# Layer-normed rows turned by one DMA per batch instead of by TensorE, and probabilities of two heads turned by one DMA

## The reference, cut to what matters

```python
h = jnp.maximum(_layernorm(x), 0.0)                  # no gain, no bias
q, k, v = split_heads(h @ Wq.T), split_heads(h @ Wk.T), split_heads(h @ Wv.T)
a = einsum('bhnd,bhmd->bhnm', q, k) * 512 ** -0.5 + (adj + adj)[:, None]
row_nonzero = any(a != 0, axis=-1)
p = softmax(where(row_nonzero, a, -inf)); p = where(isnan(p), 0, p)
o = einsum('bhnm,bhmd->bhnd', p, v)                  # heads put side by side
return x + o @ Wo.T
```

## Time and profile before

| | us |
|---|---|
| median of three runs (lowest, highest) | 1005.39 (1004.05, 1005.59) |
| the profiled execution's own time | 1005.16 |
| its span in the profile | 1003.4 |
| busy: PE, ACT, POOL, DVE | 959.6, 934.5, 862.3, 850.0 |
| transposing DMAs issued: heads, weights | 512, 4 |

### The profile page before, as it was taken

One profiled execution on the slowest core, in us unless ns is written; L12 is line 12 of the kernel. 1 busy time (PEld: TensorE's weight loads), 2 busy tenths in 40 slices (PEclk: granted clock), 3 DMA queues, 4 the chain that ended last, 5 costly groups with the idle time before them and its releaser, 6 DMA issues.

```text
span 1003.4 us, 33752 instructions
## 1 busy us (share of the span) xinstructions
PE 959.6 (96%) x11580; PEld 660.2 (66%) x11580; DVE 850.0 (85%) x3092; ACT 934.5 (93%) x3049; POOL 862.3 (86%) x936
## 2 busy tenths in 40 slices
PE   5879999999999999999999999999999999999965
PEld 4656776666677666777666677766666776667632
DVE  6778998888989888898988889988889898888863
ACT  5799999999999999999999999999999999999992
POOL 2278998989998898999888899989889988889894
PEclk9989999999999999999999999999999999999979
DMA  6289999999999999999999999999999999999995
GB/s 251 49 148 195 183 190 194 183 193 186 190 191 184 195 178 187 194 199 180 192 177 198 183 203 184 189 194 178 198 183 197 186 191 193 177 185 176 175 175 119
DMA packets 573818, 183.62 MB, mean 183 GB/s; under 512 B 547024, under 2 KB 555216, under 8 KB 573648
## 3 DMA queue, kind: packets, MB, share of 16 engines
q1 hardware_dynamic: 573648, 181.48, 100.9%
HBM read 29.36 MB, written 16.78 MB: 46 GB/s over the span
## 4 chain that ended last, share of the span: by engine, by line
PE 56%; DVE 28%; issue 8%; ACT 5%; POOL 1%; DMA 1%; DVEq 0%; POOLq 0%; ACTq 0%; SPq 0%
PE ps L1045 35%; DVE logits L752 15%; PE ps L1113 9%; PE ps L1063 7%; DVE stats L649 4%; ACT probs L547 3%; PE ps L942 3%; DVE q_lo L815 2%; DVE o_norm L782 2%; PE ps L1089 1%; DVE some L770 1%; ACT p L560 1%; PE ps L1019 1%; DMA w_nat<-in_L_gnn_Wq 1%; DVE row_min L752 1%
## 5 line engine op out<-in xcount | busy, mean ns | idle before, releaser
L430 POOL TENSOR_TENSOR p<-probs,p 128x512 f16<-128x512 f32 x512 | 586.4, 1161 | 89.9 <-ACT p L560 89.7
L547 ACT ACTIVATE probs<-logits,row_min 128x256 f32<-128x256 f32 x1024 | 513.6, 511 | 3.8 <-DVE row_min L752 3.8
L752 DVE CUSTOM_DVE_ANT_0 logits<-ps,adj_s,sigma 128x256 f32<-128x256 f32 x1024 | 438.0, 475 | 7.1 <-PE ps L1063 7.0
L560 ACT ACTIVATE p<-probs 128x512 f16<-128x512 f32 x512 | 323.5, 632 | 0.0
L1045 PE MATMUL ps<-ht_hi,w_hi 128*128 128x256 f16 x1024 | 280.2, 274 | 7.7 <-DVE q_lo L815 2.6
L1045 PE MATMUL ps<-ht_lo,w_hi 128*128 128x256 f16 x1024 | 279.4, 273 | 0.0
L1045 PE MATMUL ps<-ht_hi,w_lo 128*128 128x256 f16 x1024 | 279.4, 273 | 0.0
L547 ACT ACTIVATION_READ_ACCUMULATOR probs<-logits,row_min 128x1 f32 x1024 | 209.8, 205 | 0.0
L1045 PE MATMUL ps<-wo,o_hi 128*128 128x512 f16 x496 | 149.2, 383 | 3.8 <-POOL o_lo L456 3.8
L1045 PEld LDWEIGHTS ps<-ht_hi,w_hi 128*128 128x128 f16 x1024 | 100.1, 98 | 36.1 <-DVE q_lo L815 13.0
L1045 PEld LDWEIGHTS ps<-ht_lo,w_hi 128*128 128x128 f16 x1024 | 100.4, 98 | 14.0
(11 more groups left out here) (90 smaller groups left out, 1571.0 us busy)
## 6 DMA issues: line engine op xcount, KB each, us to landing
xs<-in_x SPq DMA_DIRECT2D x32, 512.0 KB, 4.6
out<-xs SPq DMA_DIRECT2D x64, 256.0 KB, 2.9
adj_raw<-in_adj SPq DMA_DIRECT2D x32, 256.0 KB, 3.2
pt<-p SPq DMA_TRANSPOSE x256, 4.0
w_nat<-p SPq DMA_TRANSPOSE x256, 3.4
w_nat<-in_L_gnn_Wq SPq DMA_DIRECT2D x2, 512.0 KB, 5.4
w_nat<-in_L_gnn_Wk SPq DMA_DIRECT2D x1, 1024.0 KB, 8.3
w_nat<-in_L_gnn_Wv SPq DMA_DIRECT2D x1, 1024.0 KB, 11.3
```

What stands on the lines that cost most here:

```text
L430: g.tensor_tensor(p16[:, c % 2, k, 1], probs[:, h % 4].rearrange("p u n -> p (u n)"), p16[:, c % 2, k, 0], ALU.subtract).then_inc(p_split, 1)
L547: e = a.activation(probs[:, h % 4, u, :], logits[:, h % 4, u, :], ACT.Exp, bias=row_min[:, t.par(d), u, h:h + 1], scale=-1.0, accum_out=ro ...
L560: a.activation(p16[:, c % 2, k, 0], probs[:, h % 4].rearrange("p u n -> p (u n)"), ACT.Copy)\
L752: v.tensor_tensor_reduce(out=logits[:, h % 4, u, :], in0=ps[:, S_BANK + h % HC, N * u:N * u + N], in1=adj_s[:, t.par(d), u, :], scale=sigm ...
```

## The change

Batches 0, 1 and 2 are still turned by PE; batches 3 to 31 (`H_TURNED` = 3, `h_by_dma`) are split into hi and lo before they are turned, and one DMA turns both halves of both row tiles (128 x 2048 float16). The probabilities of heads 2i and 2i+1 are turned by one DMA of 128 x 2048 instead of two of 128 x 1024. For the batches from 3 on:

- POOL writes `xn` = max(x - mean, 0) at s = 3, without the factor; the factor is applied when the rows are rounded. POOL also takes over the scaled variance from DVE (`var_s`), and the negated mean is gone.
- At s = 5 ACT rounds row tile 0 to float16 with the factor, and POOL row tile 1 (`round_h` of each), into `h16`, which lies in the storage of the third weight.
- DVE writes the lo halves at s = 6 (tile 0) and s = 10 (tile 1) (`rest_of_h`).
- At s = 11 SP waits for both and issues the one DMA into `ht`. PE's job 0 of the next slot waits for it.
- `turn_h` on PE and both `take_h` (ACT and DVE) are gone for these batches.

`ht` holds both halves and both tiles, in pieces of 128 columns; where a matmul streamed 256 columns of `ht_hi` that lay side by side it now streams two pieces of 128.

The diff below is cut; its parts come in this order: constants and tiles, SP, POOL (`layernorm`, then its `round_h`), the one instruction of ACT's `round_h`, DVE (`ln_mean_var`, then `rest_of_h`), PE. The added lines of `wait_ge` are shown for SP, POOL and PE; ACT's `round_h` has the same three waits as POOL's.

```diff
+H_TURNED = 3
+H_BY_ACT = (0,)
+H_HI_STEPS, H_LO_STEPS = (5, 5), (6, 10)
+        h16 = w16[:, 2]
-        neg_mean = sb("neg_mean", [P, NU])
-        ht_hi = sb("ht_hi", [P, 2, NC, N], F16)
-        ht_lo = sb("ht_lo", [P, 2, NC, N], F16)
+        ht = sb("ht", [P, 2, NU, 2 * NC, P], F16)
...
+        def h_rows_free(eng, b):
+            if b == H_TURNED:
+                eng.wait_ge(wo16_in, 16 * NC)
+            else:
+                eng.wait_ge(ht_in, 16 * (b - H_TURNED))
...
-                if d is None or not by_dma(h):
+                if d is None or h % 2 == 0:
                     return
-                c, k = h // HC, h % HC
+                c, k = h // HC, h % HC - 1
                 sp.wait_ge(p_split, x_count(t.batch(d), h) + 1)
                 need(sp, pv_done, 2 * t.batch(d) + c // 2 - 1)
-                sp.dma_start_transpose(pt(c, k), p16[:, c % 2, k].rearrange("p l n -> p (l n)"))\
-                  .then_inc(pt16_in[c][k], 16)
+                sp.dma_start_transpose(pt_two(c, k), p16[:, c % 2, k:k + 2].rearrange("p k l n -> p (k l n)"))\
+                  .then_inc(pt16_in[c][k // 2], 16)
...
+                    if s == 11 and later(t, 2) and h_by_dma(t.batch(2)):
+                        b = t.batch(2)
+                        sp.wait_ge(h_split, NU * (b - H_TURNED + 1))
+                        sp.wait_ge(pj_full, NJ * t.batch(0) + 6)
+                        sp.dma_start_transpose(ht[:, b % 2].rearrange("p u l n -> p (u l) n"),
+                                               h16[:, 0:NU].rearrange("p u n -> p (u n)")).then_inc(ht_in, 16)
...
-                pool.wait_ge(ln_stats, NU * (t.batch(d) + 1))
+                pool.wait_ge(stat_step, 2 * NU * (b + 1))
+                if h_by_dma(b - 1):
+                    pool.wait_ge(h_split, NU * (b - H_TURNED))
+                g.tensor_scalar(var_s[:], mean_var[:, :, 1], EPS, 2.0 ** (-2 * H_UP), ALU.add, ALU.mult)\
+                 .then_inc(var_ready, 1)
+                pool.wait_ge(var_ready, b + 1)
                 g.tensor_tensor(rstd[:], var_s[:], minus_half[:], ALU.pow).then_inc(rstd_ready, 1)
...
+                    if h_by_dma(b):
+                        g.tensor_scalar(xn[:, u, :], xs[:, b % X_RING, u, :], mean_var[:, u, 0:1], 0.0,
+                                        ALU.subtract, ALU.max).then_inc(xn_ready, 1)
+            def round_h(b, u):
+                pool.wait_ge(xn_ready, NU * b + u + 1)
+                pool.wait_ge(rstd_ready, b + 1)
+                h_rows_free(pool, b)
+                g.tensor_scalar(h16[:, u, 0:D], xn[:, u, :], rstd[:, u:u + 1], 1.0, ALU.mult, ALU.mult)\
+                 .then_inc(h_hi_pool, 1)
...
+                a.activation(h16[:, u, 0:D], xn[:, u, :], ACT.Copy, scale=rstd[:, u:u + 1]).then_inc(h_hi_act, 1)
...
-                v.tensor_scalar(neg_mean[:], mean_var[:, :, 0], -1.0, None, ALU.mult).then_inc(ln_stats, 1)
-                v.tensor_scalar(var_s[:], mean_var[:, :, 1], EPS, 2.0 ** (-2 * H_UP), ALU.add, ALU.mult)\
-                 .then_inc(ln_stats, 1)
+            def rest_of_h(b, u):
+                v.scalar_tensor_tensor(out=h16[:, u, D:2 * D], in0=xn[:, u, :], scalar=rstd[:, u:u + 1],
+                                       in1=h16[:, u, 0:D], op0=ALU.mult, op1=ALU.subtract).then_inc(h_split, 1)
...
-                                        HT[b][:, t.par(1), kc, :], i == 0, i == len(steps) - 1))
+                                        ht[:, t.par(1), :, NC * b + kc, :], i == 0, i == len(steps) - 1))
...
-                    if j == 0:
+                    if j == 0 and h_by_dma(t.batch(1)):
+                        pe.wait_ge(ht_in, 16 * (t.batch(1) - H_TURNED + 1))
+                    elif j == 0:
                         pe.wait_ge(aux_taken, aux_after("h", t.batch(1), 1))
...
-                    for k in range(HC):
+                    for k in range(HC // 2):
                         pe.wait_ge(pt16_in[c][k], 16 * (t.batch(d) + 1))
```

More of the change, by code:

```diff
@@ L172, in emit @@
         stat_step = sem("stat_step")
-        ln_stats = sem("ln_stats")
+        var_ready = sem("var_ready")
+        h_hi_act = sem("h_hi_act")
+        h_hi_pool = sem("h_hi_pool")
+        h_split = sem("h_split")
+        ht_in = sem("ht_in")
         rstd_ready = sem("rstd_ready")
@@ L190, in emit @@
         p_split = sem("p_split")
-        pt16_in = [[sem(f"pt16_in{i}{k}") for k in range(HC)] for i in range(NC)]
+        pt16_in = [[sem(f"pt16_in{i}{k}") for k in range(HC // 2)] for i in range(NC)]
         v_hi_ready = sem("v_hi_ready")
@@ L230, in emit @@
             for at, key in sorted(slot_uses):
+                if key[0] == "h" and h_by_dma(key[1]):
+                    continue
                 if 0 <= key[1] < NB and not (key[0] == "y" and key[2] not in Y_C):
@@ L304, in h_turns, with h_parts @@
             at = (10, 13) if t.first else (5, 8)
-            return [k for k in range(2) if at[k] == s and later(t, 2)]
+            return [k for k in range(2) if at[k] == s and later(t, 2) and not h_by_dma(t.batch(2))]
         def h_rests(t, s):
             at = (10, 13) if t.first else (6, 10)
-            return [k for k in range(2) if at[k] == s and later(t, 2)]
+            return [k for k in range(2) if at[k] == s and later(t, 2) and not h_by_dma(t.batch(2))]
+        def h_parts(t, s, steps):
+            return [u for u in range(NU) if steps[u] == s and later(t, 2) and h_by_dma(t.batch(2))]
+        def h_rows_free(eng, b):
[3 more added lines that the diff above has]
+                eng.wait_ge(ht_in, 16 * (b - H_TURNED))
         first = Slot(0, -1, False, False, True)
@@ L485, in slot @@
                         layernorm(t, 2)
+                    for u in h_parts(t, s, H_HI_STEPS):
+                        if u not in H_BY_ACT:
+                            round_h(t.batch(2), u)
                     if s == 7 and t.nxt:
@@ L630, in slot @@
                         take_h(t.batch(2), k)
+                    for u in h_parts(t, s, H_HI_STEPS):
+                        if u in H_BY_ACT:
+                            round_h(t.batch(2), u)
             run(act, slot)
@@ L652, in ln_mean_var @@
                 step = 2 * NU * t.batch(d)
+                need(dve, xn_ready, NU * t.batch(d))
                 for u in range(NU):
@@ L862, in slot @@
                             take_h(t.batch(2), k)
+                        for u in h_parts(t, s, H_LO_STEPS):
+                            rest_of_h(t.batch(2), u)
                     for b, u in residuals(t, s):
@@ L939, in turn_h @@
                     need(pe, aux_taken, aux_before("h", b, k))
-                for c in range(2):
-                    for u in range(NU):
-                        m = tr(ps[:, bank, N * c + P * u:N * c + P * u + P],
-                               xn[:, u, P * (2 * k + c):P * (2 * k + c) + P], ident[:])
+                for c in range(NC):
+                    m = tr(ps[:, bank, P * c:P * c + P], xn[:, k, P * c:P * c + P], ident[:])
                 m.then_inc(aux_full, 1)
@@ L982, in _ @@
             W = (w_hi, w_lo)
-            HT = (ht_hi, ht_lo)
             O = (o_hi, o_lo)
```

42 lines of the change are left out of this document (29 added, 13 removed).

## The result

The changed kernel takes 1093.12 us (median of four runs, 1091.75 to 1093.65) against 1005.36 before: ratio 1.087, interval 1.086 to 1.089. It is 8.7% slower; 977 was forecast. The profiled execution has a span of 1090.0 us.

A forecast was written before the change was run, and what follows sets the result against it. PE was taken as the bound at 29.51 us a slot, ACT and POOL close behind. ACT would bind next; with waits 28.5 us, 1.0 less over 29 slots: 1005.16 - 29.3 + 0.8 = 976.7, so 977, range 964 to 1003.

The forecast's parts named there:

- POOL, `xn`: POOL's normalized rows lose one of two per-row factors: 767 ns towards 687 each, counted with an ended wait as -0.25 us.
- the prediction's own sum: POOL's work per slot: 27.16 + 0.65 + 0.3 - 0.25 = 27.86 us, upper end 28.9.
- Rival 2: POOL binds at 28.9 us a slot, or late splits in steps 6 to 9 hold ACT: 988 to 995; chance 0.20.
- The prediction's own sign of being wrong: Wrong if ACT waits for POOL's splits over 0.3 us a slot, or PE shows waits for `ht` or `pt`.
- DVE's lo halves: DVE's two lo halves per slot, now read from SBUF: 0.69 to 0.89 us each.
- SP and the DMAs: A DMA of 128x2048 was taken to hold SP 2.5 us and land 4.9 us after issue.
- 22.5 us ... it fits: SP's nine big DMAs a slot take 22.5 us, plus about 2.3 for four plain ones, within 28.3.
- margin of 0.3 us at PE's step 0: The rows' DMA lands at 516.8, before PE begins step 0 at 517.1.
- rival 3: Turned rows land late and PE waits 2.3 us a slot: 1032, deciding from 1.4 us of wait; chance 0.13.
- The pairing: Paired head DMAs change nothing by themselves in the slots; the last pair's later landing adds 0.8 us at the end.
- PE and ACT: Per slot, PE needs 28.08 us and ACT, the new bound, 28.27; with waits a slot is 28.5.
- PE's 0.40 us for q's lo half: PE's wait per slot for DVE's lo half of q goes, as DVE drops the negated mean and scaled variance.

The follow-up runs named there:

- e4: Kernel before, with POOL subtracting the mean in `xn` instead of adding the negated mean; 1058.30 us, ratio 1.053.
- e5: Kernel before, with a series of twelve kinds of POOL instruction on 128x512, four of each, put ahead of POOL's work; 1078.67 us in one execution.
- e6: e1 with the max of `xn` replaced by a multiplication by 1.0, so no ReLU for batches 3 to 31; 1030.84 us, ratio 1.025.
- e1: Changed kernel, with DVE writing the negated mean again and POOL adding it instead of subtracting the mean; 1086.49 us, ratio 1.080.
- e9: Changed kernel, with POOL's `xn` kept to add and mult and ACT rounding both row tiles with the ReLU at step 5; 1025.40 us, ratio 1.021.
- e2: Kernel before, with only the paired DMAs for the probabilities of two heads; 1007.26 us, ratio 1.002.
- e13: e10 with the rows' DMA and PE's wait for it left out, PE projecting from stale rows; 978.52 us, ratio 0.974.
- e15: Kernel before, with the negated mean and scaled variance moved from DVE to POOL, in mult and add alone; 996.05 us, ratio 0.991.
- e3: Changed kernel, with one DMA a head again instead of one for two heads; 1100.09 us, ratio 1.094.
- e14: Kernel before, with DVE's `ln_mean_var` moved from step 2 to step 3, behind q's lo half; 1006.66 us, ratio 1.001.
- e10: e9 with the second input of DVE's lo half in PSUM, so the lo halves are not those of h; 1024.11 us, ratio 1.020.
- e8: Changed kernel, with POOL's `xn` kept to add and mult; ACT rounds row tile 0 and DVE row tile 1 with the ReLU; 1027.08 us, ratio 1.021.

## Why the prediction was wrong

- **POOL, `xn`** (the step that failed first): "from 767 ns towards 687 each". It went to 1998. The price was taken from a row with the same shape but other operations: the kernel before held no tensor-scalar with subtract or max on POOL, so the trace did not show it, and the prediction should have bounded it from above as it did the rounding (1.16). With even 1.16 it would still have been short: no row of POOL on 128x512 came near 2.0. Put into the prediction's own sum, 27.86 + 2 x 1.31 = 30.5 us, past every other engine; with 0.4 for the adjacency, 0.3 for the splits and 0.7 of waits for ACT that remain it is 31.9, where the slot shown took 32.02. e4, e5 and e6 show the operation alone, by itself and taken away: 56 of e1's 81 us went with it.
- **Rival 2** was the right mechanism (POOL behind in steps 3 to 9, ACT waiting for its splits, as it now does for 3.0 us a slot) with the wrong size, 28.9 us where it is 32.0; it was given 0.20 and priced at 988 to 995. The prediction's own sign of being wrong, ACT waiting for the splits by more than 0.3 us a slot, is what came.
- **DVE's lo halves**: the forecast 0.69 to 0.89 us each were 0.96 in the changed kernel and 1.09 to 1.27 in the corrected ones. The term was mis-sized, and what it does to POOL (the adjacency, 687 to 1090 ns) was not in the sum at all. The upper bound of 0.89 was the mean of four instructions of which three took 0.76 us at most and one 1.29. The long one began early in a split of POOL and ended 0.55 us after it; the others began when a split had 0.1 to 0.2 us left. So the trace of the kernel before had the effect in it, and the mean hid it. Their least, median and most, and the timeline of that one:

```profile
L679 DVE SCALAR_TENSOR_TENSOR w_nat<-w_nat,w_scale x4: 752/756/1285, 58.4 to 66.1; 128x512 f16<-128x512 f32 x4
```

```profile
58.02 1.16 POOL L430 TENSOR_TENSOR p<-probs,p 128x512 f16<-128x512 f32 x1
58.45 1.28 DVE L679 SCALAR_TENSOR_TENSOR w_nat<-w_nat,w_scale 128x512 f16<-128x512 f32 x1 [2.42 <-ACT w_nat L520]
```

- **SP and the DMAs**: the 2.5 us on SP were 2.4 to 3.6 at the median, and the 4.9 us to landing 5.3 and 6.0. "22.5 us ... it fits" failed: in e9 SP issues without a pause for a slot of 30.2 us ((1024.4 - 1003.4) / 29 + 29.51). The margin of 0.3 us at PE's step 0 did not hold: PE waited for the rows in seven of eight slots of the changed kernel, half a microsecond a slot on average (4.2 us in eight), not the 1.4 that rival 3 needed.
- **The pairing** costs nothing in the slots (e2), as forecast. The 1.2 us of span at the end, where 0.8 was taken, are right by luck: the late landing itself delayed nothing, and the last projection ran at the lower clock.
- **PE and ACT**: no run has their forecast work without the other costs. The nearest, e13, has a slot of 28.54 us with neither waiting, but with ACT's second rounding in it; the agreement with 28.5 is in part luck.
- **PE's 0.40 us for q's lo half** goes when the two small instructions leave DVE (e15, 8.5 us won). Their price of 0.55 us, from the earlier trace rows, was for the most part waiting for POOL: the same instruction takes 0.17 us where no instruction of POOL is running.
- The figure of the Trainium skill ("VectorE: DVE Perf Modes", "The three transpose paths"), set aside with an estimate of 21 us for 16 tiles, gives too much here too: they land in 6.0 us at the median. Its advice (same page, "Rules for kernel authors"), to turn on TensorE where PSUM will do, was right in this kernel, for other reasons than the time of one transpose: the volume comes on top of 16 other units, and DVE's inputs move from PSUM to SBUF.

What stays open: why the paired DMAs gain 7 us where POOL binds (e3), how the DMAs' limit divides between SP's issuing and the engines behind it, and what e14's order is worth with the negated mean off DVE; none was tried.

## What to carry to other kernels

Price an instruction by a row with its engine, its shape and its operations; where one of the three has no row, measure it alone before it goes on an engine that has no slack, or stay with operations that the trace shows. Read a group's least, median and most and not its mean alone: a wide spread on one shape says that a wait is inside the instruction's time. When work moves from PSUM to SBUF inputs on DVE, look at what POOL does at that time. And when taking away one suspected cost changes little, take away the two next bounds together before giving either up: here each alone won 1 to 4 us and both won 47.

## What the runs showed of the hardware

- On POOL a tensor-scalar on 128x512 float32 takes 0.70 us (mult, mult) or 0.77 (add, mult), and 1.92 to 2.08 as soon as either operation is subtract or max (e5). Tensor-tensor add, subtract and mult all take 1.04.
- DVE and POOL wait for each other's instructions where DVE's is a scalar-tensor-tensor with both inputs in SBUF. With 128x512, 49 of 58 began well inside an instruction of POOL and ended 0.54 to 0.55 us after its end (e9); the mean is 1.27 us, against 0.68 with one input in PSUM (e10). With 128x8, 67 of 128 began so in the kernel before and ended within 0.06 us of its end; with none beside it one takes 0.11 to 0.12 us. POOL's rounding takes 1.06 us instead of 0.62 where it waits for such an instruction of DVE (e9).
- A DVE tensor-scalar with its one input and its output in SBUF waits too: the negated mean on 128x2 (0.17 us alone, up to 1.1 beside POOL; kernel before, e14), and the rounding with the ReLU in e8 (0.95 us on average), of which 19 of 29 began well inside an instruction of POOL and ended 0.28 us or more after it.
- The time at which a transposing DMA frees SP depends on load: for 128x2048 from 1.3 to 4.8 us in the changed kernel.
